# Third attention: a second exponential of every second group moves from ScalarE to VectorE, its score taken early into a tile of its own

## The reference, cut to what matters

```python
def _L1_attn_b_ref(x):                     # x: 4 x 1024 x 128, 16 heads of 8
    xh = x.reshape(B, T, H, hd)
    x_centered = xh - jnp.mean(xh, axis=1, keepdims=True)
    corr = jnp.einsum('bthd,bThd->bhtT', x_centered, x_centered)
    corr = jax.nn.softmax(corr, axis=-1)
    out = jnp.einsum('bhtT,bThd->bthd', corr, xh)
    return out.reshape(B, T, D)
```

## Time and profile before

| | |
|---|---|
| time, median of 3 runs | 3331.67 us (3326.85 to 3334.49) |
| the profiled execution | 3326.8 us, span 3325.1 us |
| third attention, first to last exponential on ScalarE | about 2784 to 3249 us of the span |
| busy share of the span | PE 86%, ACT 71%, DVE 70%, POOL 7% |
| in that attention (2901 to 3016 us) | ACT 114.42 of 115 us, PE 101.16, DVE 52.74 |
| granted TensorE clock | mean 0.943 of full speed |

### The profile page before, as it was taken

One profiled execution on the slowest core, in us unless ns is written; L12 is line 12 of the kernel. 1 busy time (PEld: TensorE's weight loads), 2 busy tenths in 40 slices (PEclk: granted clock), 3 DMA queues, 4 the chain that ended last, 5 costly groups with the idle time before them and its releaser, 6 DMA issues. The chain is left out here.

```text
span 3325.1 us, 53184 instructions
## 1 busy us (share of the span) xinstructions
PE 2864.9 (86%) x17952; PEld 1289.8 (39%) x17952; DVE 2341.3 (70%) x3808; ACT 2377.3 (71%) x3572; POOL 221.9 (7%) x177
## 2 busy tenths in 40 slices
PE   4788888899999578888889999979979756888886
PEld 2221221566766311111147667742237641111115
DVE  6677777677676767777767777779999855444454
ACT  5689889555465579999955545556635657999994
POOL 2000000100000310000010000010000011000002
PEclk8899999999999789999989999989989967999997
DMA  5445453000000444445300000000000004233321
GB/s 113 70 58 74 64 68 49 26 0 0 0 0 1 118 99 60 64 55 70 54 31 0 0 0 0 0 27 1 1 1 0 0 22 103 38 55 51 57 49 29
DMA packets 76712, 125.47 MB, mean 38 GB/s; under 512 B 12936, under 2 KB 28200, under 8 KB 75628
## 3 DMA queue, kind: packets, MB, share of 16 engines
q1 hardware_dynamic: 76492, 122.65, 21.7%
HBM read 87.49 MB, written 29.16 MB: 35 GB/s over the span
## 5 line engine op out<-in xcount | busy, mean ns | idle before, releaser
L1931 ACT ACTIVATE m_mix_hidden<-m_mix_up_ps 128x512 f32<-128x512 f32 x512 | 305.6, 597 | 295.5 <-PE m_mix_up_ps L1847 295.5
L1114 ACT ACTIVATE b_direct_probs<-b_direct_s_ps 128x1024 f32<-128x1024 f32 x512 | 473.6, 1094 | 17.7 <-PE b_direct_o_ps L1021 11.9
L1855 PE MATMUL m_mix_down_ps<-m_w,m_mix_hidden 128*128 128x128 f32 x4096 | 474.8, 276 | 0.0
L1855 PEld LDWEIGHTS m_mix_down_ps<-m_w,m_mix_hidden 128*128 128x128 f32 x4096 | 467.2, 192 | 15.3 <-issue 15.3
L1847 PE MATMUL m_mix_up_ps<-m_mix_ZT,m_w 128*128 128x512 f32 x1024 | 472.1, 619 | 0.0
L1114 ACT ACTIVATE a_direct_probs<-a_direct_s_ps 128x1024 f32<-128x1024 f32 (+10 forms) x512 | 431.8, 938 | 52.8 <-DVE a_direct_s_ps L1152 39.8
L1114 ACT ACTIVATE c_att_probs<-c_att_s_ps 128x1024 f32<-128x1024 f32 x496 | 457.9, 1148 | 6.7 <-PE c_att_s_ps L997 4.2
L1149 DVE TENSOR_TENSOR b_direct_s_ps<-b_direct_s_ps,distance 128x512 f32<-128x512 f32 x512 | 335.7, 695 | 142.4 <-PE b_direct_s_ps L997 141.5
L1152 DVE SCALAR_TENSOR_TENSOR a_direct_s_ps<-distance,slopes,a_direct_s_ps 128x512 f32<-128x512 f32 (+3 forms) x512 | 355.5, 732 | 113.3 <-PE a_direct_s_ps L997 102.0
L1021 PE MATMUL c_att_o_ps<-c_att_probs,c_v_cols 128*32 128x512 f32 x1984 | 274.3, 609 | 50.6 <-ACT c_att_probs L1114 50.6
L1021 PE MATMUL b_direct_o_ps<-b_direct_probs,v_cols 128*32 128x512 f32 x2048 | 275.1, 610 | 14.0 <-DVE b_direct_taken L1138 13.1
(11 more groups left out here) (385 smaller groups left out, 3486.2 us busy)
## 6 DMA issues: line engine op xcount, KB each, us to landing
qk_parts<-b_qkv_parts SPq DMA_DIRECT2D x48, 256.0 KB, 3.9
qk_parts<-a_qkv_parts SPq DMA_DIRECT2D x24, 256.0 KB, 3.7
a_k_rows<-qk_parts SPq DMA_DIRECT2D x32, 192.0 KB
a_q_rows<-qk_parts SPq DMA_DIRECT2D x32, 192.0 KB
b_k_rows<-qk_parts SPq DMA_DIRECT2D x32, 192.0 KB
b_q_rows<-qk_parts SPq DMA_DIRECT2D x32, 192.0 KB
qk_parts<-c_split_parts SPq DMA_DIRECT2D x24, 256.0 KB, 3.0
c_k_rows<-qk_parts SPq DMA_DIRECT2D x32, 192.0 KB
```

What stands on the lines that cost most here:

```text
L1114: act.activation(probs[:, J % 2, j, lo:hi], s_ps[:, slot(hg, place), lo:hi], ACT.Exp).then_inc(exped, 1)
L1855: last = pe.matmul(down_ps[:, t % 2, e, :], hidden[:, e * HALVES + h, t * P:(t + 1) * P], w["w2"][:, e * HALVES + h, :], start=(h == 0), s ...
L1931: act.activation(hidden[:, f, :], up_ps[:, f % UP_BANKS, :], ACT.Silu).then_inc(silu_done, 1)
```

## The change

`given` becomes a tuple per group: groups 0 and 2 of a batch still give one unit (31) to VectorE, groups 1 and 3 give two (31 and 30). The given units stand at places 2 and 6 (`GIVEN_AT`). `KEPT` and `GIVEN`, the counts of units before a group, become lists, and every wait is rewritten with them. `power` and `raised` get one part for each given unit of a group, and VectorE takes the second score right after it has copied the right sums, ahead of the raising of the first; it rounds and raises the second after the first.

```diff
-    ORDER = [n for n in range(UNITS) if n not in given]
-    KEPT = len(ORDER)
-    NE = HG * KEPT
-    NG = len(given)
-    GIVEN_AT = (2, 15)[:NG]
-    for place, n in zip(GIVEN_AT, given):
-        ORDER.insert(place, n)
+    given = given or ((),) * HG
+    GIVEN_AT = (2, 6)
+    ORDER = [[n for n in range(UNITS) if n not in units] for units in given]
+    KEPT = [sum(len(order) for order in ORDER[:hg]) for hg in range(HG + 1)]
+    NE = KEPT[HG]
+    GIVEN = [sum(len(units) for units in given[:hg]) for hg in range(HG + 1)]
+    NG = GIVEN[HG]
+    for order, units in zip(ORDER, given):
+        for place, n in zip(GIVEN_AT, units):
+            order.insert(place, n)
...
-            power = k.sb(f"{tag}_power", [P, SEQ])
+            power = k.sb(f"{tag}_power", [P, max(len(units) for units in given), SEQ])
...
-            raised = k.sb(f"{tag}_raised", [P, NG, SEQ])
+            raised = k.sb(f"{tag}_raised", [P, max(len(units) for units in given), SEQ])
...
-                if ORDER[was] in given:
-                    pe.wait_ge(powers_out, b * (NG * HG) + (of * NG + given.index(ORDER[was]) + 1))
+                unit = ORDER[of][was]
+                if unit in given[of]:
+                    pe.wait_ge(powers_out, b * NG + (GIVEN[of] + given[of].index(unit) + 1))
                 else:
-                    pe.wait_ge(exped, b * NE + (of * KEPT + ORDER[was] + 1 + SLOTS))
+                    pe.wait_ge(exped, b * NE + ((KEPT[of] if of >= 0 else KEPT[HG - 1] - NE) + unit + 1 + SLOTS))
...
-                    pe.wait_ge(exped, b * NE + (hg * KEPT + min(GH * (J + 1), KEPT) + SLOTS))
-                    if given and J == JT - 1:
-                        pe.wait_ge(raised_out, b * (NG * HG) + (hg + 1) * NG)
+                    pe.wait_ge(exped, b * NE + (min(KEPT[hg] + GH * (J + 1), KEPT[hg + 1]) + SLOTS))
+                    if given[hg] and J == JT - 1:
+                        pe.wait_ge(raised_out, b * NG + GIVEN[hg + 1])
...
@@ def batch(b, first, final):
                             round_power(*after, 0)
                         take_sums(b, hg, 1)
+                        for i in range(1, len(given[after[1]]) if following else 1):
+                            take_power(*after, i)
                         if following:
                             raise_two(*after, 0)
                         if hg == 1 and not first:
                             invert(b - 1, 0)
                             invert(b - 1, 1)
-                        for i in range(1, NG if following else 1):
-                            take_power(*after, i)
+                        for i in range(1, len(given[after[1]]) if following else 1):
                             round_power(*after, i)
                             raise_two(*after, i)
...
         attend_transposed(nc, f"{tag}_att", XN, operands, joined, ident, X=X, kept=const.kept_sums,
-                          given=(TPB * GH - 1,))
+                          given=((TPB * GH - 1,), (TPB * GH - 1, TPB * GH - 2)) * (HEADS // GH // 2))
```

More of the change, by code:

```diff
@@ L979, in scores @@
             def scores(hg, place, b):
-                J, j = divmod(ORDER[place], GH)
+                J, j = divmod(ORDER[hg][place], GH)
                 half = hg % 2
@@ L1019, in sum_up @@
                         n = J * GH + j
-                        weights = raised[:, given.index(n), lo:hi] if n in given else probs[:, J % 2, j, lo:hi]
+                        weights = raised[:, given[hg].index(n), lo:hi] if n in given[hg] else probs[:, J % 2, j, lo:hi]
                         last = pe.matmul(o_ps[VW * j:VW * (j + 1), c, lo - c * BANK:hi - c * BANK],
@@ L1102, in batch @@
                 for hg in range(HG):
-                    for place, n in enumerate(ORDER):
-                        if n in given:
+                    for place, n in enumerate(ORDER[hg]):
+                        if n in given[hg]:
                             continue
@@ L1166, in round_power @@
                     dve.wait_ge(raised_out, at)
[L1167 removed]
+                dve.tensor_copy(whole[:, :], power[:, i, :]).then_inc(rounded, 1)
             def raise_two(b, hg, i):
[L1170 to L1172 removed]
+                at = b * NG + (GIVEN[hg] + i)
+                done = b * (NG * RAISE) + (GIVEN[hg] + i) * RAISE
+                rest, acc = power[:, i, :], raised[:, i, :]
                 dve.wait_ge(rounded, at + 1)
@@ L1213, in batch @@
                             invert(b, 1, 1)
-                        following = given and not (final and hg == HG - 1)
+                        following = NG and not (final and hg == HG - 1)
                         after = (b, hg + 1) if hg + 1 < HG else (b + 1, 0)
@@ L1244, in batch @@
                                 invert(b, INVERT_AT.index(n), 1)
-            for i in range(NG):
+            for i in range(len(given[0])):
                 take_power(0, 0, i)
```

14 lines of the change are left out of this document (5 added, 9 removed).

## The result

The kernel with the change takes **3361.9 us** (median of 4 runs, 3358.96 to 3369.43) against 3330.77 (3326.85 to 3334.49) for the kernel before: ratio 1.0100, 95% interval 1.0084 to 1.0115, 31 us slower. The forecast was 3367.3 in 3354 to 3381. The profiled execution took 3358.96 us, span 3357.2; against the 3325.1 of before that is +32.1.

What follows compares the result with a forecast made beforehand. ScalarE was taken as the bound, its loop through TensorE having 0.16 us spare. Profiled 3326.8 plus 35.6 (eight groups at 4.45) gave 3362.4; against the runs' median, 4.9 higher, 3367.3 us, range 3354 to 3381.

Steps and rivals of the forecast that it cites:

- What bounds: Third attention: ScalarE bounds at 0.924 us an exponential, but the loop through TensorE's product and score has only 0.16 us spare.
- The wait in each block: Changed groups: left product waits one place later, ScalarE then waits 0.76 us for scores; block 4.42 us instead of 3.66.
- 1.00 and the 0.06: TensorE: 1.00 us from product to next pair of scores, 0.06 us from end of exponential to start of product.
- start of a score to the end of its exponential: With ScalarE standing waiting: 1.53 us, read at place 5 at a group's start; 0.12 allowed either way.
- Forecast for the groups: Third attention: each of eight changed groups 4.45 us longer than 28.65, together +35.6 us.
- VectorE costs nothing: Changed groups: second take ends 1.2 us before its slot is wanted, raising 26.25 us into the group; cost zero.
- The copies stay ahead, so GpSimd and SyncE do not shift: Copies of the sums precede VectorE's added work, so GpSimd's copy of the values and SyncE's moves stay put.
- ScalarE staying the bound: Rival: score of place 4J + 7 arrives within 1.83 us, eight exponentials simply go, 3324.4 us; chance 0.04.
- The wait partly caught up: Rival: some blocks lose nothing because TensorE reaches scores earlier, half the waits remain, 3345.6 us; chance 0.05.
- VectorE late: Rival: second take or raising overruns its margin, delaying a slot or last product, about 3375 to 3385 us; chance 0.03.
- TensorE's clock: Rival: clock falls in the changed groups, 69 us for all blocks, 35 if down half the time, 3402 us; chance 0.06.
- ScalarE's idle time: Sign: idle before the third attention's exponentials rises from 6.7 to some 50 us, put down to scores.

Runs made afterwards that it cites:

- those with the products one step later: The change with left and right products of blocks 0 to 5 called one step later in groups with two given units: 3330.41 us, ratio 1.0001.
- The spare work alone: Kernel before, its score order kept; VectorE also scales, rounds and raises on unread spare tiles in groups 1 and 3: 3333.72 us, ratio 1.0009.
- the faster kernels: The change giving units 19 and 31, products of blocks 0 to 3 one step later: in groups 1 and 3 3329.5 us, in all 16 groups 3320.6.
- One and the same kernel: The change with units 19 and 31 given, products of blocks 0 to 3 one step later, groups 1 and 3: 3329.5 us; profiled twice.
- second unit at place 15: The change with the second given unit at place 15 instead of 6, taken after the first is raised: 3355.17 us, ratio 1.0082.

## Why the prediction was right, point by point

- **What bounds**: right. The loop of exponential, product, score, exponential had 0.16 us to spare and became the bound. Of the kernels whose units stand two places back, only those with the products one step later had ScalarE as the bound again.
- **The wait in each block**: the mechanism, its place and its number of blocks right, its size a little off. Forecast 2.59 us from the end of place 4J + 5 to that of 4J + 7; measured 4.34 - 1.83 = 2.51. Of its terms 1.00 and the 0.06 stand; the mis-sized one is "start of a score to the end of its exponential", taken as 1.53 from place 5 at the start of a group. It is 0.43 + 1.02 = 1.45. At place 5 ScalarE had only just ended another exponential and the instruction has a second wait, for the sums of two blocks earlier; here it stood idle. Which of the two made the 0.08 was not tried. Seven waits in eight groups make 4.5 us, and the 0.12 that the prediction allowed covered it.
- **The end of a batch**: overlooked. In before, three of the eight groups to be changed already ended with a wait of 0.6 to 0.7, as the 0.68 of the earlier trace rows; the pauses absorbed it, 3 x 0.65 = 2 us less. Forecast for the groups +35.6, measured +29.2; of the difference of 6.4 some 4.4 are the term above and 2.0 this.
- **The loop's edge** (+0.9, TensorE's clock) was not forecast either, nor what lies ahead and behind, +2.0. These 2.9 run against the 6.4 above, so the profiled execution is only 3.4 us below its sum (3358.96 against 3362.4). That part of the closeness is luck.
- **VectorE costs nothing**: right. The second take ended at 2820.18, 1.2 us ahead of the score that wants its slot (2821.36); the raising ended 25.7 us behind the first take, as worked out (2898.20 - 2872.47). The spare work alone came out at +0.09%, with an interval that includes zero.
- **"The copies stay ahead, so GpSimd and SyncE do not shift"**: incomplete. The inversion of the last batch's sums did move behind the second raising. It cost nothing in the change, since its group had become longer than the raising; in the faster kernels it cost 1.9 us.
- **The rivals.** ScalarE staying the bound: refuted, at 2.51 against 1.83. The wait partly caught up: refuted, blocks 1 to 6 of every changed group pay. VectorE late: refuted in the change, and seen where the take stood behind a raising. TensorE's clock: refuted for the blocks; PEclk is 1.00 from 2815 to 3016 us with 1.20 us of waiting in each block of 4.34. The Trainium skill's rule (TensorE: Matmul & The Clock Gate, A second HAM failure mode: psum-queue depth-cycling), by which such bursts make the clock swing, is not borne out there. The clock did fall once in this attention, at the loop's edge behind 2.50 us of idle time, where the prediction had not looked.
- **ScalarE's idle time** was forecast as some 50 us and is 38.0, 0.57 a pause instead of 0.76. A block lost 4.34 - 3.66 = 0.68. Of that 0.11 does not show as idle time: four exponentials behind a pause take 3.77, and four in an unbroken row end 3.66 apart, each beginning while the one ahead is still recorded as running; the first behind a pause has none ahead of it. The idle time of a group of instructions is less than what the waits cost.

## What to carry to other kernels

Taking work off a full engine pays only if the loop through that engine has room: add up the round trip of exponential, product and score before counting the saved instruction. Where an in-order queue feeds the full engine, a wait that moves one place later holds back everything behind it, and an item put in early moves every later wait; move the waiting instruction by the same number of places and choose the given items so that the shift ends soon. And once a stage gets shorter, look at what used to be covered by it at its end.

## What the runs showed of the hardware

- VectorE's operations on two tiles in SBUF slow down beside GpSimd's: four steps of 128 x 1024 take 7.07 us with a 2.74 us multiplication of GpSimd beside them, and 5.00 without. In the kernel before, the last step of the last raising takes 3.28 us instead of 1.23 beside such a multiplication of 2.81. The Trainium skill says that the two share their interfaces to SBUF, with contention for VectorE's instructions with two SBUF inputs (GPSIMD Engine Reference, Specifications); the rows agree, and give it a size.
- The matmuls of the next scores did not pass a product that waited. In the change the slot of the next score comes free one exponential ahead of the end of the product's wait (at 2822.20 us, against 2823.12), and yet the score follows the left product's start by 1.00 us (2824.17), in this block as in the others shown.
- One and the same kernel differed by 5.7 us between two executions in the last 80 us alone, where TensorE's granted clock was 0.70 and 0.79. That is nearly a fifth of the 31 us under study; differences of 0.2% in this kernel are read from a stretch of the trace rather than from the total.
- TensorE's clock held at 1.00 with a wait of 1.20 us in every block of 4.34, and fell behind single idle times of 2.50 us (the change, 0.60 from 3036 to 3040 us) and 3.16 us (second unit at place 15, 0.50 from 3258.2 to 3262 us). Idle times of 2.43 us (before) and 2.31 us (VectorE's work alone) had no fall and a fall behind them, so the length alone does not decide it.
- The recorded duration of an exponential grows from 1.02 to 1.29 us in an uninterrupted row while one ends every 0.92 us. The distance of the ends, and not the mean duration, is the rate.
